# Routed experts: up loads that wait for their slot's own expert and go out six blocks ahead, and two copies moved ahead of Gelu

## What is computed

```python
x = x + scan(ctx, layernorm(x))          # conv, softplus, 16 states, gate
h = layernorm(x)
aff = sigmoid(h @ wa);  p, i = top_k(aff, 2);  p = p / sum(p)
expert(h) = (gelu(h @ g + gb) * (h @ w1 + b1)) @ w2 + b2
x = x + sum of 2 shared experts + sum over the 2 picked experts of p * expert_i(h)
```

## Time and profile before

| | |
|---|---|
| median of 3 runs | 870.52 us (869.25 to 873.93) |
| the profiled execution | 866.54 us, span 864.8 us |
| mean granted clock of TensorE | 0.969 |
| PE busy | 776.5 us, 90% of the span |
| DVE, ACT, POOL busy | 700.6, 543.8, 566.2 us |

### The profile page before, as it was taken

How to read it: one execution, slowest core, us unless ns; L and a number is a source line. 1 busy time by engine, 2 the same in 40 slices (tenths; PEclk the granted TensorE clock), 3 DMA queues, 4 the chain that set the end, 5 groups by cost and what they waited for, 6 DMA issues and landing times.

```text
span 864.8 us, 15422 instructions
## 1 busy us (share of the span) xinstructions
PE 776.5 (90%) x4431; PEld 599.8 (69%) x4431; DVE 700.6 (81%) x859; ACT 543.8 (63%) x883; POOL 566.2 (65%) x348
## 2 busy tenths in 40 slices
PE   6963699999999989999899999999999999999992
PEld 3622688888888878888778778886666665666651
DVE  4999999989998998999777677736777776776671
ACT  3887799999999999997243522033544445554440
POOL 9552299989999999999845542032447557555422
PEclk9967799999999999999999999999999999999997
DMA  6010311111141213100320112238378887777763
GB/s 186 1 54 2 98 61 53 60 49 63 50 158 51 60 40 110 58 29 3 146 97 2 49 50 98 74 131 356 53 214 205 211 224 190 209 179 181 202 146 49
DMA packets 35399, 91.83 MB, mean 106 GB/s; under 512 B 8716, under 2 KB 9228, under 8 KB 32000
## 3 DMA queue, kind: packets, MB, share of 16 engines
q1 hardware_dynamic: 23360, 65.50, 22.4%
q0 software_dynamic: 11968, 25.44, 14.8%
HBM read 122.24 MB, written 21.36 MB: 166 GB/s over the span
## 4 chain that ended last, share of the span: by engine, by line
PE 45%; DVE 16%; ACT 10%; SPq 9%; issue 8%; POOL 6%; DMA 4%; DVEq 0%; ACTq 0%; POOLq 0%
DVE r L1057 9%; PE ps L1458 7%; PE ps L1460 7%; PE ps L1459 7%; POOL r L528 5%; PE ps L1561 4%; PE ps L1584 4%; PE ps L1816 4%; ACT mem L769 3%; ACT r L754 3%; SPq L390 2%; SPq L392 2%; PE ps L1562 2%; SPq L391 2%; PE ps L1797 2%
## 5 line engine op out<-in xcount | busy, mean ns | idle before, releaser
L528 POOL TENSOR_TENSOR r<-r,mem 128x1024 f32<-128x1024 f32 x127 | 297.5, 2378 | 34.4 <-DVE r L1057 34.1
L1057 DVE TENSOR_TENSOR_SCAN r<-r,ps 128x1024 f32<-128x1024 f32 x128 | 286.2, 2276 | 9.0 <-issue 8.4
L754 ACT ACTIVATE r<-mem,nega 128x511 f32<-128x511 f32 x256 | 166.6, 713 | 1.1 <-DVE r L1057 1.0
L1561 PE MATMUL ps<-ident,mem 128*128 128x128 f32 x768 | 130.5, 279 | 27.8 <-DVE r L1057 20.8
L1584 PE MATMUL ps<-ident,r 128*128 128x128 f32 x1024 | 132.5, 273 | 3.7 <-DVE r L1087 2.4
L769 ACT ACTIVATE mem<-mem,b_turned 128x512 f32<-128x512 f32 x192 | 124.7, 714 | 8.8 <-PE ps L1562 8.5
L1561 PEld LDWEIGHTS ps<-ident,mem 128*128 128x128 f32 x768 | 87.4, 142 | 53.0 <-issue 52.1
L1584 PEld LDWEIGHTS ps<-ident,r 128*128 128x128 f32 x1024 | 115.9, 141 | 4.3 <-DVE r L1087 2.6
L1382 DVE TENSOR_TENSOR acc_again<-r,acc_again 128x1536 fp32r<-128x1536 f32 x47 | 82.7, 1760 | 44.3 <-ACT acc_again L912 42.2
L1562 PE MATMUL ps<-mem 128*128 128x128 f32 x512 | 100.0, 277 | 0.0
L1458 PE MATMUL ps<-split 128*128 128x512 f32 x216 | 87.2, 404 | 2.6 <-issue 1.1
(11 more groups left out here) (206 smaller groups left out, 1284.9 us busy)
## 6 DMA issues: line engine op xcount, KB each, us to landing
r<-in_r_up SPq DMA_DIRECT2D x47, 1024.0 KB
mem<-in_r_down SPq DMA_DIRECT2D x47, 512.0 KB
mem<-cm_rows SPq DMA_DIRECT2D x64, 256.0 KB, 3.3
mem<-in_r_b SPq DMA_DIRECT2D x4, 2048.0 KB, 12.4
out<-acc POOLq DMA_DIRECT2D x17, 256.0 KB, 7.0
r<-in_x SPq DMA_DIRECT2D x4, 1024.0 KB, 4.9
xn_scratch<-r SPq DMA_DIRECT2D x16, 256.0 KB, 2.8
mem<-in_ctx_t SPq DMA_DIRECT2D x4, 512.0 KB, 7.0
```

What stands on the lines that cost most here:

```text
L528: pool.tensor_tensor(state[:, k % 2, ec:ec + 2], state[:, k % 2, ec:ec + 2], c, ALU.mult).then_inc(s["weighed"], 1)
L754: act.activation(decay[:, k % 2, ec, 1:L], delta[:, b, ec, 1:L], ACT.Exp, scale=nega[:, ec, n:n + 1]).then_inc(s["decay_ready"], 1)
L1057: dve.tensor_tensor_scan(state[:, half, ec:ec + 2].rearrange("p e l -> p (e l)"), decay[:, half, ec:ec + 2].rearrange("p e l -> p (e l)"), ...
L1561: pe.transpose(ps[:, ec, lt * P:(lt + 1) * P], dbu_t[:, k % 2, lt, ec * P:(ec + 1) * P], ident[:])
```

## The change

An up load no longer waits for block j-4's product. DVE writes a further list, blk_lead: the number of blocks that end with the last block of the expert that held the slot before, at most j-3 and at least 1. The up load reads it as a fourth register number, waits for h_ready to reach it, and first for the up load four before it on the same semaphore to have landed. AHEAD goes from 3 to 6, so the queue's order is up 4 to 9, then down j and up j+6 in turn. The loop is gone: all loads stand in straight code. In the shared stage ACT copies two turned tiles ahead of Gelu 3, and ahead of Gelu 9, and DVE makes the rests of the first two before hidden tile 3.

```diff
-AHEAD = 3
+AHEAD = 6
...
             def load_up(j, r):
-                if not isinstance(j, int) or j >= SLOTS:
-                    wait_apart(sp, s["h_ready"], j - SLOTS + 1)
+                if j >= SLOTS:
+                    sp.wait_ge(s[f"up_{r}"], 16 * (j // RING))
+                    done = sp.value_load(blk_lead[0:1, j:j + 1], min_val=1, max_val=NBLK)
+                    wait_apart(sp, s["h_ready"], done)
                 load(up_w, r_up, "up", j, r)
 
             def load_down(j, r):
-                if not isinstance(j, int) or j >= SLOTS:
-                    wait_apart(sp, s["o_ready"], j - SLOTS + 1)
+                if j >= SLOTS:
+                    sp.wait_ge(s["o_ready"], j - SLOTS + 1)
                 load(down_w, r_down, "down", j, r)
...
-            for j in range(1, RING):
-                load_up(j + AHEAD, (j + AHEAD) % RING)
-            with sp.Fori(1, (NBLK - 2) // RING) as jj:
-                for r in range(RING):
-                    load_down(RING * jj + r, r)
-                    load_up(RING * jj + r + AHEAD, (r + AHEAD) % RING)
-            for j in range((NBLK - 2) // RING * RING, NBLK):
+            sp.wait_ge(s["blocks_ready"], 3)
+            for j in range(SLOTS, SLOTS + AHEAD):
+                load_up(j, j % RING)
+            for j in range(SLOTS, NBLK):
                 load_down(j, j % RING)
                 if j + AHEAD < NBLK:
                     load_up(j + AHEAD, (j + AHEAD) % RING)
...
+            turn_normed(1, range(2))
             gelu(3)
-            turn_normed(1, range(2))
...
+            turn_normed(3, range(2))
             gelu(9)
-            turn_normed(3)
+            turn_normed(3, range(2, LT))
...
+            def list_leads():
+
+                three_up, blocks = blk_new[0:1], blk_cmp[0:1]
+                dve.wait_ge(s["blocks_ready"], 2)
+                dve.tensor_scalar(three_up, blk_e[0:1], 3.0, None, ALU.add).then_inc(s["run_made"], 1)
...
             hidden_rests(1)
+            token_rests(1, range(2))
             hidden_shared(3)
-            token_rests(1, range(2))
...
             add_shared(2, range(2, LT))
+            list_leads()
```

More of the change, by code:

```diff
@@ L256, in bass_xattn_scan_moe_kernel @@
         row_ids = blk_run
+        blk_lead = sb("blk_lead", [P, NBLK], I32)
         blk_load = sb("blk_load", [P, NBLK], I32)
@@ L1255, in list_ids @@
                 dve.tensor_scalar(row_ids[:], ps[:, SIDE_BANK[0], 0:NBLK], pad_f[:, 0:1], None, ALU.add).then_inc(s["bar_made"], 1)
+            def list_leads():
+                three_up, blocks = blk_new[0:1], blk_cmp[0:1]
+                dve.wait_ge(s["blocks_ready"], 2)
+                dve.tensor_scalar(three_up, blk_e[0:1], 3.0, None, ALU.add).then_inc(s["run_made"], 1)
+                dve.wait_ge(s["run_made"], 4)
+                dve.tensor_tensor(blocks, iota_f[0:1, 0:E].unsqueeze(1).to_broadcast([1, NBLK, E]),
+                                  three_up.unsqueeze(2).to_broadcast([1, NBLK, E]), ALU.is_le).then_inc(s["run_made"], 1)
+                dve.wait_ge(s["run_made"], 5)
+                dve.tensor_tensor(blocks, blocks, nblk[0:1].unsqueeze(1).to_broadcast([1, NBLK, E]), ALU.mult).then_inc(s["run_made"], 1)
+                dve.wait_ge(s["run_made"], 6)
+                dve.tensor_reduce(blk_f[0:1], blocks, AX_X, ALU.add).then_inc(s["run_made"], 1)
+                dve.wait_ge(s["run_made"], 7)
+                dve.tensor_scalar(blk_f[0:1], blk_f[0:1], float(NBLK), -1.0, ALU.subtract, ALU.mult).then_inc(s["run_made"], 1)
+                dve.wait_ge(s["run_made"], 8)
+                dve.scalar_tensor_tensor(out=blk_f[0:1], in0=three_up, scalar=E - 1.5, in1=blk_f[0:1],
+                                         op0=ALU.is_lt, op1=ALU.mult).then_inc(s["run_made"], 1)
+                dve.wait_ge(s["run_made"], 9)
+                dve.scalar_tensor_tensor(out=blk_f[0:1], in0=iota_f[0:1, 0:NBLK], scalar=float(1 - SLOTS), in1=blk_f[0:1],
+                                         op0=ALU.add, op1=ALU.min).then_inc(s["run_made"], 1)
+                dve.wait_ge(s["run_made"], 10)
+                dve.tensor_scalar(blk_lead[0:1], blk_f[0:1], 1.0, None, ALU.max).then_inc(s["blocks_ready"], 1)
             def list_waits():
```

## The result

| | before | changed kernel |
|---|---|---|
| median of 13 runs each | 870.32 us (865.74 to 874.72) | 866.78 us (863.77 to 870.63) |
| ratio, 95% interval | | 0.9962 (0.9944 to 0.9980) |
| the profiled execution | 866.54 us, span 864.8 | 866.65 us, span 864.9 |

3.5 us less by the medians, 0.38% by the ratio. A later measurement of the same kernel gave 0.9999 (0.9983 to 1.0015), and the two intervals don't meet. So they don't cover what changes from one measurement to the next, and the two leave the gain open between none and some 0.4%. The two profiled executions are equally long, so the profile shows exchanged waits, not a gain.

What follows compares the result with a forecast made beforehand. It took SyncE's own instruction stream, 5.68 us a block against PE's 5.33, as the bound late in the last stage. Terms of -0.5 and -1.4 made -1.9, from 870.5 to 868.6 us; 8-in-10 range 863.0 to 877.0.

Steps and rivals of the forecast that it cites:

- little change: Whole kernel: the likeliest case, 866.1 to 874.8 us, late up weights coming back as late down weights; chance 0.42.
- Up loads gain 3 blocks, 16 us, and the 6.9 us of lateness goes: Routed experts' stage: up loads issued six blocks ahead end PE's 6.9 us of stalls, if SyncE keeps up.
- 5.6 us a pair: SyncE in the routed experts' stage: time to issue one up and one down load, bounds 5.4 and 5.9 us.
- 815.5 for down load 40: SyncE's queue, routed experts' stage: down load 40 issued at 815.5 us, 36 pairs after down load 4 at 613.9.
- Landing "5.5": Down load 40: 5.5 us from issue to landing, floor 3.0, ceiling 6.5; its product then waits 5.5 us.
- From about block 27 on, some 5 us in all: Sign in the profile after: PE idle before down products, ended by the down weights' DMA, some 5 us.
- -1.9 us: Sum for the routed experts' stage: product 40 starts 0.5 us sooner and block 43's 1.4 us stall goes.
- a store chain that binds only at the end: Rival: output scatters, 4.73 to 4.9 us apart, stretch past PE's 5.33; gain near 0, 870 us; chance 0.05.
- Gain 0.5: Shared stage: two copies ahead of Gelu on ACT shorten PE's idle times by 0.5 us, between 0 and 1.9.
- The full gain of 7.4 us at a shorter pair: Rival, routed experts' stage: below 5.45 us a pair all stalls vanish, 863.1 us at best, up to 866.1; chance 0.32.
- The outright slower rival: SyncE becomes the bound from a pair of 5.77 us; at 5.9, +8.9 us, 879.4; chance 0.21.
- theory B: Theory of the experiments: earlier up loads crowd scatters and gathers around blocks 13 to 17, where PE waits for a gather.

Runs made afterwards that it cites:

- e1: The changed kernel run again without an edit; 867.7 us, ratio 0.9999 to the kernel before.
- e2: The changed kernel with the shared stage's copies and rests back in the old order, leaving only the loads' part; ratio 0.9989 to the kernel before.
- e6: The changed kernel with up weights loaded eight blocks ahead instead of six; ratio 1.0037 to the kernel before.
- e9: The changed kernel, six ahead, with down loads reusing registers their block's up load read, four register loads a pair instead of seven; ratio 0.9947 to the kernel before.
- e5: The changed kernel with up weights loaded four blocks ahead instead of six; ratio 0.9926 to the kernel before.
- e8: The changed kernel with weights loaded for the first four experts only, SyncE visiting every load as before; ratio 0.9893 to the kernel before.
- e11: The changed kernel with up weights loaded five blocks ahead instead of six; ratio 0.9943 to the kernel before.
- e3: The kernel before with only the shared stage's new order, loads as before; ratio 1.0015 to the kernel before.
- e4: The changed kernel with both weights of a block loaded in one SyncE visit, after both products of the slot's last expert; ratio 0.9993 to the kernel before.
- e12: The changed kernel with up weights four blocks ahead, e5 measured once more; ratio 0.9927 to the kernel before.
- e10: The changed kernel with registers kept from up to down load as in e9, but four blocks ahead; 865.16 us, ratio 0.9954 to the kernel before.
- e7: e4 with an added wait meant to keep loads at most six blocks ahead of their block; ratio 0.9985 to the kernel before.

## Why the prediction was right, and where it wasn't

866.8 us lies 1.8 below the forecast and in its range, and "little change" was the likeliest case. Its mechanism, late up weights exchanged for late down weights, is shown by e1, e2, e6 and, by its absence, e9. It wasn't the whole of it: in the one execution of the changed kernel that was first profiled no down weights were late at all, and a gather cost about as much. That the two are of one size is luck.

1. "Up loads gain 3 blocks, 16 us, and the 6.9 us of lateness goes": nearly. Up load 24 gained 14.3 us (from 706.48 to 692.20; 11.6 in e1), which was enough. ACT's wait for them is gone in the changed kernel, e1 and e2.
2. "5.6 us a pair": right, 5.62. But I took it as one number for the kernel. The same kernel had 5.72 in e1, other orders 5.57 (e6) to 5.73 (e5), and with little traffic it was 5.50 (e8). At 0.1 us for 3.6 us at block 40, that spread is as large as what an order gains.
3. "815.5 for down load 40": 814.54 in the first profile, 818.69 in e1. Landing "5.5": at block 40 of e1 PE started 5.9 us after the load went out, but at its other waits up to 8.6 (block 22), and in e11 7.5, above my ceiling of 6.5. The long ones mostly had an expert's up load just ahead in the queue: up load 27 for down load 22 in e1. With four ahead the pairs are 29 and 32, 34 and 37, 40 and 43, and the down products of 29, 34 and 40 are those that waited in e5. No run isolates this. "From about block 27 on, some 5 us in all": from block 22 on, 5.7 us, in e1; none in the first profile, where that sign of mine failed.
4. The sum, "-1.9 us", had no term for the gathers, and this is the step that failed. I read the earlier trace rows as a store chain that binds only at the end, and gave it 0.05. In the changed kernel it cost 7.4 us in one execution and 2.9 in another. The forecast came out right since that stall takes the place of late down weights in part: 7.5 lost in the one profile, 8.7 in the other, 6.9 before.
5. The list, "4.1 us, cost nothing": 3.9 us (561.48 to 565.41), and PE shows no idle time for it.
6. "Gain 0.5" in the shared stage: 0.47 in the trace. e3 can't tell it from 0.
7. The full gain of 7.4 us at a shorter pair: e9 has the shorter pair and the stalls for weights gone, but 0.9947, 4.4 us by the medians. The rest went to a gather, 7.1 us in the profile, an execution 1.9 us longer than the median.
8. The outright slower rival, decided by SyncE's pace: it didn't come true at six ahead, but at eight, 1.0037, where the down loads stand two up loads further back.

**Shown:** without the transfers of weights neither kind of stall comes (e8); the length of SyncE's visits decides whether weights are late (e4, e9 against e1); the order chooses which (e3, e5, e6). **Open:** which transfer meets which scatter. Late gathers came in all kernels with six or eight ahead that move all weights and in those with short visits, and in none of before, e3, e5, e11 and e12. So they go with earlier loads, as theory B says, and no run refutes it. But the up loads aren't the whole of it. In e4 up load 13 went out 1.5 us later than in e5, where no gather was late, and down load 13 went out 16.5 us earlier (639.74 and 656.28). Read over all profiles, gathers were late where up load 13 went out before 632 us or down load 13 before 654, and in no other kernel. That was read afterwards, from one profile each, and it doesn't give the size: with both loads later than the changed kernel's by 1.2 and 3.1 us e1 lost 2.9 us, and e6, with its up load 3.3 us earlier and its down load 9.7 us later, lost 1.8, where the changed kernel lost 7.5. No run moves one kind of load alone. Nor was a kernel tried whose gathers stand ahead of the waiting scatter on GpSimd.

The best version is four ahead, the change with one number different: 0.9926 and 0.9927 in two measurements on two chips, 5.5 and 6.0 us faster than before by the medians. Five ahead, 0.9943, can't be told from it. It has 0.74 of the 1.07% that e8 shows to be had.

## What to carry to other kernels

A queue that issues without waiting and still falls behind is limited by its own instructions. Loading earlier in such a queue only takes time from what stands behind, so shorten the visit or choose the order by the time left to each load. A shorter visit also sends every load earlier, and here that came with late gathers (e4, e9, e10), so look at what the loads then meet. Try the neighbours of the number: here 3 (the kernel before), 4, 5, 6 and 8 ahead gave 1, 0.993, 0.994, 0.996 to 1.000 and 1.004. When an experiment adds a wait, read in the trace whether the loads went out any later before you conclude from the time: in e7 they didn't. Where two sources of lateness lie in one loop, the longer hides the other, and taking one away shows its value only once both are gone.

## What the hardware showed beyond that

A wait of PE costs more than its length once the clock falls. Idle times of 3.60, 4.12, 3.88 and 2.96 us (changed kernel, e9, e11, e7) cost 7.4, 7.0, 5.75 and 5.3 us of the block, with a granted clock of 0.58, 0.61, 0.70 and 0.74 from PE's restart to the next closing pair, a part of it at the lower level of 1.2 GHz: in e11 the first split matmul behind the wait took 1.41 us and the next 0.63, where the block before has 0.80 and 0.40. Idle times of 1.67 us (e1) and 2.69 us (e4) left the clock at 1.00 and cost 2.3 and 3.4. The window of e9, 665 to 671 us:

```profile
665.00:671.00 6.00, 5.62 (x12) 3.19 (x13) 1.70 (x3) 2.59 (x5) 2.32 (x2) 0.52 0.35 77
```

The Trainium skill (TensorE: Matmul & The Clock Gate, HAM oscillation — how this bites in real kernels) says that a wait for a DMA between bursts of matmuls puts the clock back to half, so that the next burst runs cold. The changed kernel's trace agrees, with 3.78 us for four matmuls that take 1.88; the shorter waits of e1 and e4 did no such thing.

SyncE's visits, some 3.1 and 2.5 us for an up and a down load, are about half of 5.9 us, the shortest time from a down load's issue to a product that waited for it in e1, and are paid too where a load moves nothing. The Trainium skill (DMA: Bandwidth & Descriptors, Issuing engines are not separate DMA queues) calls the time to start a DMA usually small beside the DMA itself. With three or four register loads ahead of each that isn't so here, as e9 against e1 shows.
